# Log counts added to the attention scores in place of a mask product and a count factor, with value frames made on chip, key parts stored once, later loads of the gated stage's weights, and new orders on all engines

## The reference

```python
# 1: attention of 16 heads of width 16 over the 64 picked rows (a row may be picked more than once)
q = (layernorm(x) @ W_q.T)
c_sel = (ctx @ W_kv_down.T)[indices]
k, v = c_sel @ W_kv_up.T
attn = softmax(q . k / 4, over the 64 picks)
x = x + (attn @ v) @ W_out.T
# 2: gated linear attention of 8 heads of width 64: a dense part and one of 4 experts by a router
q1, k1, v, q2, k2 = products of layernorm(x);  k2 = softmax(k2)
gk1, gk2 = log_sigmoid(...) / 16              # decays, per token and channel
o = chunk_gla(q1, k1, v, gk1) + sum_e chunk_gla(q2 * fac_e, k2 * fac_e, v, gk2 * mask_e)
x = x + (rmsnorm(o) * norm_w * silu(g)) @ Wo
```

## Time and profile before

| what | value |
|---|---|
| median of 3 runs | 1254.29 us (1249.91 to 1254.9) |
| the profiled execution | 1254.05 us, span of its instructions 1252.6 us, so 1.45 us lie around it |
| TensorE matmul / weight load busy | 1171.6 us (94%) / 952.0 us (76%) |
| VectorE busy | 980.0 us (78%), 2026 instructions |
| ScalarE busy | 913.4 us (73%) |
| GpSimd busy | 640.3 us (51%) |
| chain that ended last | PE 85%, DMA 5%, SyncE's queue 3%, ACT 3%, DVE 2% |
| DMA | 74.82 MB, mean 60 GB/s |

### The profile page before, as it was taken

The page is one execution under the profiler, slowest core; times in us unless marked ns, Lnnn a source line. Parts: engine busy times, 40 slices in busy tenths (PEclk is TensorE's granted clock), DMA queues, the critical chain, the costliest instruction groups (busy, mean ns, idle before and its releaser), DMA issues.

```text
span 1252.6 us, 30881 instructions
## 1 busy us (share of the span) xinstructions
PE 1171.6 (94%) x12256; PEld 952.0 (76%) x12256; DVE 980.0 (78%) x2026; ACT 913.4 (73%) x2290; POOL 640.3 (51%) x632
## 2 busy tenths in 40 slices
PE   2668999999999999999999999999999999999986
PEld 1446878788887777888888788888887888878864
DVE  3655888888888888888888888888888888877642
ACT  2365778778777877777778778777787787777751
POOL 2413455655544655554456555544565555445553
PEclk7877999999999999999999999999999999999998
DMA  8233112222221222122212221222222212212111
GB/s 285 69 72 98 49 49 59 49 55 72 59 56 41 58 53 54 37 53 64 83 45 58 49 55 40 53 59 51 83 58 49 59 38 52 59 39 52 30 25 23
DMA packets 82246, 74.82 MB, mean 60 GB/s; under 512 B 33017, under 2 KB 66239, under 8 KB 82102
## 3 DMA queue, kind: packets, MB, share of 16 engines
q1 hardware_dynamic: 81670, 71.89, 22.6%
q10 hardware_dynamic: 432, 0.95, 0.2%
HBM read 39.98 MB, written 15.52 MB: 44 GB/s over the span
## 4 chain that ended last, share of the span: by engine, by line
PE 85%; DMA 5%; SPq 3%; ACT 3%; DVE 2%; POOL 1%; issue 1%; ACTq 0%; POOLq 0%; DVEq 0%
PE F L391 15%; PE F L737 5%; PE TA L684 5%; PE F L385 5%; PE F L789 5%; PE F L764 5%; PE F L725 5%; PE F L800 4%; PE F L655 3%; PE SA L673 3%; PE SA L678 3%; PE F L794 3%; PE MA L691 3%; PE F L960 3%; PE TA L385 2%; PE F L781 2%
## 5 line engine op out<-in xcount | busy, mean ns | idle before, releaser
L1334 POOL TENSOR_TENSOR ZREST<-HID,ZPARTS 128x128 f32<-128x128 f32 x32 | 13.8, 431 | 218.9 <-ACT ZPARTS L1205 218.9
L1365 POOL TENSOR_TENSOR LS<-LS,ZABS 128x1024 f32<-128x1024 f32 x32 | 75.5, 2359 | 58.0 <-ACT ZABS L1278 58.0
L673 PE MATMUL SA<-MASK,minus 128*128 128x308 bf16 x256 | 73.0, 298 | 22.0 <-DMA QS<-q_dram 20.7
L665 DVE TENSOR_REDUCE PACKED<-HOT 128x19 int32<-128x1216 bf16 x64 | 92.2, 1441 | 0.1
L1321 POOL CAST IW<-IDX 128x64 f32<-128x64 int32 x32 | 8.0, 250 | 160.9 <-DMA IDX<-idx_dram 160.9
L684 PE MATMUL TA<-CONST,EXPS 128*128 128x128 f32 x512 | 87.6, 294 | 0.8 <-ACT OT L1270 0.8
L1355 POOL TENSOR_TENSOR QM<-QD,ISEXPT 128x1024 f32<-128x1024 f32 x32 | 75.9, 2372 | 5.0 <-DMA QD<-QG 4.9
L684 PEld LDWEIGHTS TA<-CONST,EXPS 128*128 128x128 f32 x512 | 72.0, 209 | 6.5 <-issue 5.1
L1357 POOL TENSOR_TENSOR AT<-AT 128x1024 f32<-128x1024 f32 x32 | 75.9, 2371 | 0.8 <-DVE AT L1055 0.8
L1358 POOL TENSOR_TENSOR QM<-QD,ISEXPT 128x1024 f32<-128x1024 f32 x32 | 76.0, 2375 | 0.0
L678 PE MATMUL SA<-KNOW,QS 128*128 128x154 bf16 x512 | 73.1, 232 | 0.0
(11 more groups left out here) (269 smaller groups left out, 3958.7 us busy)
## 6 DMA issues: line engine op xcount, KB each, us to landing
QD<-QG SPq DMA_DIRECT2D x128, 128.0 KB, 2.4
QS<-q_dram SPq DMA_DIRECT2D x64, 192.0 KB, 3.2
q_dram<-QPARTS SPq DMA_DIRECT2D x32, 192.0 KB, 2.1
XA<-x_dram SPq DMA_DIRECT2D x32, 128.0 KB, 2.2
QS<-q_dram SPq DMA_DIRECT2D x32, 128.0 KB, 2.4
XB<-x_dram SPq DMA_DIRECT2D x32, 128.0 KB, 3.0
out_dram<-OUT SPq DMA_DIRECT2D x32, 128.0 KB, 1.7
...
```

The lines of the kernel that those rows point to most:

```text
L665: return dve.tensor_reduce(PACKED[:, r], HOT[:, r, :], AX.X, ALU.add)
L673: pe.matmul(SA[:, i, 0:2 * NKV], minus[:, :], MASK[t % 2][:, :].unsqueeze(1).to_broadcast([P, 2, NKV]), start=True, stop=False, skip_group ...
```

## The change

- The counts enter the scores. ScalarE takes `LN` = Ln(COUNT + 1e-30); GpSimd makes `OFF` (-1e30 where the count is 0) and `LNC` = LN + OFF. VectorE no longer reduces a group's scores with one instruction: for each of the four heads a `tensor_tensor_reduce` adds LNC to the 154 scores in PSUM, writes them back negated in place, and keeps their minimum. In the instruction list this is a pair: one over 154 columns and one that writes the 128x1 result. The exponentials take the scores with scale -1. The mask products, `minus`, `count_transposes`, `COUNTR`, `COUNTT` and `MASK` go, and with them the factor on the transposed exponentials: `PT` is one plain copy of 640 columns across two banks, on VectorE for groups 0 and 2 and on ScalarE for groups 1 and 3.
- The value frames are made on GpSimd; `v_frame` and its four loads go.
- Each key part is stored once (three stores for batch 0, one for the other batches together), and the slabs are read with four loads per batch (`K_RUNS`).
- The loads of the weights of stages c and d move from iteration 0 to iteration 1, behind the first keys and queries.
- The order of work within an iteration is new on all five queues.

The core of the diff:

```diff
-K_SLABS = (0, 0, 0, 1, 1, 1, 2, 2)
+K_SLABS = (0, 1, 0, 1, 2, 1, 2, 0)
+K_RUNS = ((0, 2), (2, 5), (5, 7), (7, 8))
...
-        k_dram = nc.dram_tensor("k_dram", (B * P, HA * NKV), bf16).ap()
+        k_dram = nc.dram_tensor("k_dram", (B * PARTS * DA, HA * NKV), bf16).ap()
...
+        ROWS = TM[:, :, :].rearrange("p a c -> p (a c)")[:, 0:(GH + 1) * P]
+        OUTS = MA[:, 3 * P:4 * P]
...
+        def value_ones(v):
+            ones = v[:, 0:HA * VW].rearrange("p (h w) -> p h w", w=VW)[:, :, DA]
+            rest = v[:, HA * VW:VALW].rearrange("p (g h w) -> p g h w", h=GH, w=VW)[:, :, :, DA]
+            pool.memset(ones, 1.0)
+            return pool.tensor_copy(rest, const("quarter").unsqueeze(1).to_broadcast([P, GROUPS, GH]))
...
+            pool.memset(VALL[:, :, :], 0.0).then_inc(s_zeros, 1)
+
+        def pool_frames():
+            pool.wait_ge(s_zeros, 2)
+            for n in range(RB):
+                last = value_ones(VALL[:, n, :])
+            last.then_inc(s_frame, 1)
...
-            load(sp, s_frame, (VNOW[0][:, :], v_frame))
...
-            load(sp, s_frames, *[(VALL[:, n, :], v_frame) for n in range(RB)])
...
-        def sp_k_store(b):
+        def sp_k_store_first():
             for n in range(PARTS):
-                first, end = n * PARTS, min(n * PARTS + PARTS, len(K_SLABS))
-                sp.wait_ge(s_kparts, n + 1 if b == 0 else 2 * PARTS)
-                sp.dma_start(k_rows[b, :, first:end, :],
-                             KPARTS[:, b, n, :].unsqueeze(1).to_broadcast([P, end - first, KD * NKV])).then_inc(s_krows, 16)
+                sp.wait_ge(s_kparts, n + 1)
+                sp.dma_start(k_rows[:, n, :], KPARTS[:, 0, n, :]).then_inc(s_krows, 16)
+
+        def sp_k_store_rest():
+            sp.wait_ge(s_kparts, 2 * PARTS)
+            sp.dma_start(k_rows[:, PARTS:PARTS * B, :], KPARTS[:, 1:B, :, :].rearrange("p b n w -> p (b n) w")).then_inc(s_krows, 16)
+
+        def key_slabs(n):
+            for first, end in K_RUNS:
+                m = (n * PARTS + K_SLABS[first]) * DA
+                sp.dma_start(KNOW[n % 2][first * DA:end * DA, :, :].rearrange("p h j -> p (h j)"),
+                             k_dram[m:m + (end - first) * DA, :]).then_inc(s_batch[n % 2], 16)
 
         def sp_batch_first():
             sp.wait_ge(s_krows, 16 * PARTS)
-            sp.dma_start(KNOW[0][:, :, :].rearrange("p h j -> p (h j)"), k_dram[rows(0), :]).then_inc(s_batch[0], 16)
+            key_slabs(0)
 
         def sp_batch(n):
-            sp.wait_ge(s_krows, 16 * PARTS * B)
+            sp.wait_ge(s_krows, 16 * (PARTS + 1))
             sp.wait_ge(s_vrows, 16)
...
-        def count_transposes():
-            pe.matmul(spare[:, cols(0)], COUNT[:, 0:P], identb[:, :], start=True, stop=True)
-            return pe.matmul(spare[:, cols(1)], COUNTR[:, :, :].rearrange("p j h -> p (j h)"), identb[:, :], start=True, stop=True)
...
-                pe.matmul(SA[:, i, 0:2 * NKV], minus[:, :], MASK[t % 2][:, :].unsqueeze(1).to_broadcast([P, 2, NKV]),
-                          start=True, stop=False, skip_group_check=True)
...
-                                     start=False, stop=True, skip_group_check=True)
-            return last
...
+        def maxima(t, out):
+            for h in range(GH):
+                s = score_banks[:, h // 2, h % 2, :]
+                last = dve.tensor_tensor_reduce(s, s, LNC[t % 2][:, :], -1.0, LARGE, ALU.add, ALU.min, out[:, h:h + 1])
+            return last
...
+            return pe.transpose(MA[:, 0:P], exps[:, P:NPAD, :].rearrange("p j h -> p (j h)"), ident)
...
+                maxima(b, MAXS[:, 0, :]).then_inc(s_b_max, 1)
...
+            if 0 <= d < TILES:
+                dve.wait_ge(s_d_exp1, 4 * d + 4)
+                dve.wait_ge(s_d_k1_ps, d + 1)
+                dve.tensor_tensor(flat(KG1T[:, :, :]), D2, EN1[:, :], ALU.mult).then_inc(s_d_k1, 1)
...
+                maxima(b, MAXS[:, 1, :]).then_inc(s_b_max, 1)
...
+                dve.tensor_copy(PT[0][:, :], ROWS).then_inc(s_b_probs, 1)
...
-                dve.tensor_tensor(PR[0][:, :], MA[:, 3 * P:4 * P], COUNTT[b % 2][:, 1, :], ALU.mult).then_inc(s_b_probr, 1)
-                dve.tensor_tensor(PT[0][:, :, :], TA[:, :].rearrange("p (h q) -> p h q", h=GH), COUNTT[b % 2][:, 0, :].unsqueeze(1).to_broadcast([P, GH, P]), ALU.mult).then_inc(s_b_probs, 1)
...
+            if 0 <= a < TILES:
+                dve.wait_ge(s_a_hot, 2 * a + 1)
+                dve.tensor_tensor(HOT[:, :, :], HOT[:, :, :], WEIGHT[:, :].unsqueeze(1).to_broadcast([P, BASES, PICKS]), ALU.mult).then_inc(s_a_hot, 1)
...
+                dve.wait_ge(s_b_scores, 4 * b + 3)
+                maxima(b, MAXS[:, 0, :]).then_inc(s_b_max, 1)
+            if 0 <= c < TILES:
+                dve.tensor_reduce(RT[:, 1:2], LOGIT[:, :], AX.X, ALU.max, negate=True).then_inc(s_c_router, 1)
+            if 0 <= d < TILES:
                 dve.wait_ge(s_d_a1_ps, d + 1)
                 dve.tensor_tensor(by_head(AT1), banks_12, tri.unsqueeze(1).to_broadcast([P, 2 * NP, P]), ALU.mult).then_inc(s_d_at1, 1)
...
+                dve.wait_ge(s_d_a2_ps, d + 1)
+                dve.tensor_tensor(by_head(AT2), banks_12, TRIE[d % 2][:, :].unsqueeze(1).to_broadcast([P, 2 * NP, P]), ALU.mult).then_inc(s_d_at2, 1)
...
+                act.activation(PT[1][:, :], ROWS, ACT.Copy).then_inc(s_b_probs_act, 1)
...
+                act.wait_ge(s_a_qrest, 2 * a + 1)
+                act.activation(QPARTS[:, 1, :, :], QREST[:, :, :], ACT.Copy).then_inc(s_a_qparts, 1)
+            if 0 <= b < TILES:
+                act.wait_ge(s_b_values, 4 * b + 2)
+                act.activation(OT[:, 1, :], OUTS, ACT.Copy).then_inc(s_b_ot, 1)
...
-                act.activation(MASK[a % 2][:, :], COUNT[:, 0:NKV], ACT.Relu, bias=const("masked"), scale=MASKED).then_inc(s_a_counts_act, 1)
...
+                act.activation(LN[:, :], COUNT[:, 0:NKV], ACT.Ln, bias=const("tiny")).then_inc(s_a_lncount, 1)
...
+                pool.wait_ge(s_d_dec, d + 1)
+                pool.tensor_tensor(states, states, DEC[:, 0:NS].unsqueeze(2).to_broadcast([P, NS, DK]), ALU.mult)
+                pool.wait_ge(s_d_qd, 64 * d + 64)
+                pool.tensor_tensor(QM[:, 0, :, :, :].rearrange("p a b t -> p (a b) t"), QD[:, :, :, :].rearrange("p a b t -> p (a b) t"), ISEXPT[d % 2][:, 0, :].unsqueeze(1).to_broadcast([P, H, P]), ALU.mult)
...
                 pool.wait_ge(s_a_qparts, 2 * a + 1)
                 pool.tensor_tensor(QREST[:, :, :], QT[:, :, :], QPARTS[:, 0, :, :], ALU.subtract).then_inc(s_a_qrest, 1)
             if 0 <= d < TILES:
-                pool.wait_ge(s_d_dec, d + 1)
-                pool.tensor_tensor(states, states, DEC[:, 0:NS].unsqueeze(2).to_broadcast([P, NS, DK]), ALU.mult)
-                pool.wait_ge(s_d_qd, 64 * d + 64)
-                pool.tensor_tensor(QM[:, 0, :, :, :].rearrange("p a b t -> p (a b) t"), QD[:, :, :, :].rearrange("p a b t -> p (a b) t"), ISEXPT[d % 2][:, 0, :].unsqueeze(1).to_broadcast([P, H, P]), ALU.mult)
...
+                pool.tensor_scalar(OFF[:, :], COUNT[:, 0:NKV], 0.5, MASKED, ALU.is_lt, ALU.mult).then_inc(s_a_off, 1)
...
+                pool.tensor_tensor(LNC[a % 2][:, :], LN[:, :], OFF[:, :], ALU.add).then_inc(s_a_counts_pool, 1)
...
+                    sp_k_store_first()
+                    sp_batch_first()
+                if a == 1:
                     sp_weights2()
                     sp_weights3()
...
-                    for n in range(1, B):
-                        sp_k_store(n)
+                    sp_k_store_rest()
                     sp_v_store()
```

463 lines of the change are left out of this document (210 added, 253 removed).

## The result

| | before | after |
|---|---|---|
| median | 1253.32 us (4 runs) | 1240.93 us (4 runs, 1239.66 to 1243.95) |
| ratio, with its 95% interval | | 0.9912 (0.9892 to 0.9931) |
| span of the profiled execution | 1252.6 us | 1242.6 us |

What follows compares the result with a forecast made beforehand. In the steady part TensorE was taken to bound the kernel, at 35.93 us an iteration. From 1254.05 us, 23 for the iterations and 10 for the start were taken off, giving 1221 us, range 1202 to 1252.

Steps and rivals of the forecast that it cites:

- the place of `XN`: VectorE's list ahead of XN: XN 0.27 us later, so TensorE starts its transposes 6.45 us into the iteration, before 6.18.
- These cost nothing as long as their results are early: GpSimd's two added 154-column operations, with 17 us idle, and ScalarE's added work, with 7.8 us idle, were priced at nothing.
- the 35.17 of the sum: Forecast length of a steady iteration in us, 0.76 less than the present 35.93; 23 us over 30 iterations.
- The price of the pair: VectorE's two instructions per head in the maxima: 0.30 us a pair, so a group costs 1.19 us, 0.48 more.
- The estimate from the page's overheads: Trainium skill's overheads applied to VectorE's pair: 0.125 + 0.160 + 0.060 = 0.345 us, whole kernel 1237 us.
- The lower end of 0.30: VectorE's pair costs at least 0.30 us: 0.227 for 154 columns, from PR and QG, plus 0.07 from RT.
- The dear pair: Rival on VectorE's maxima: pair at 0.33 to 0.37 (about 1237 us) chance 0.17, to 0.41 0.10, above 0.12.
- `XN` first, `AT` second: Two places where TensorE waits for VectorE: XN's transposes at 6.45 us, then the first AT, ending at 15.51 us.
- the forecast wait of 0.36 us: TensorE ahead of the second `inner`: there at 15.17 us, waits for VectorE's first AT, goes on at 15.54.
- VectorE does not bind: Rival: VectorE's chain runs ahead of TensorE's, iteration 34.54 us, whole 1202 us; chance 0.08.
- The start: First iterations: key parts land earlier, first scores 6.8 us sooner, iteration 3's QS wait covered; 10 us (4 to 14).
- `QREST` late: Rival: GpSimd's QREST, now behind QM, delays OT by 0.4 us in each of 30 iterations; 1233 us, chance 0.10.

Runs made afterwards that it cites:

- both ways of doing so: Changed kernel with SG run earlier (ScalarE's exponential of LS ahead of two VM copies), 1217.23 us; or with SG held back until VectorE made XM, 1218.50 us.
- The run with the single reduction: Changed kernel with each group's four pairs replaced by the one reduction of the kernel before, counts left out of the scores: 1230.04 us, 0.9810.
- the useless reductions: Fastest version (early SG, QREST ahead of the decays, early XA and IDX loads) plus a 128x512 constant reduction ahead of each group's maxima: 1253.45 us, 1.0001.
- both runs above: Changed kernel with the nine weight loads back in iteration 0, 1247.18 us; kernel before with weight and value-frame loads moved to iteration 1, 1245.80 us.
- the best version: Changed kernel with SG earlier, QREST ahead of the decays, and the next tile's XA and IDX loads behind the query slabs: 1207.16 us, 0.9657.

## Why the prediction was wrong

Direction and range held; the size did not: 33 us forecast, 12.4 measured, 23 forecast for the iterations and 3.4 lost there. In its own steps:

- **The step that failed** is the place of `XN`, 6.45 us after the start: it takes every operation of VectorE ahead of `XN` at its old duration, and puts GpSimd at nothing, as in "These cost nothing as long as their results are early". The sum asks when a result of GpSimd is needed, not what it runs beside, and `SG` does not occur in it. The runs showed `XN` at 7.23: `SG`, which is needed some 26 us later, had moved onto VectorE's `K`, ahead of the first maxima and `Q`, and cost 1.0 us of the 1.39 I had taken off TensorE. Moving it away gave 23.7 us by the medians (22 by the ratios, each against its own runs of before), and both ways of doing so gave the same iteration.
- **Luck.** The 1217 us that this makes is within 4 us of the forecast, but by two errors that cancel: the quiet iteration is 0.26 us shorter than the 35.17 of the sum, some 8 us in 30, and the long iterations, which the sum does not have, cost 8.5 us.
- The kernel before showed it. `QREST` took 1.58 us beside the `HOT` product, and takes 0.67 in the new order; I wrote that half of it "may be contention" and used it for `QREST` alone. Had I laid GpSimd's row beside VectorE's for each operation that the new order moves, `SG` on `K` would have been found.
- The Trainium skill states it (SBUF — State Buffer, Who interferes with whom): a VectorE operation with two SBUF inputs and a GpSimd operation that reads SBUF contend for a shared port pair, and whichever issues second is blocked to the end of the first. The traces agree in both orders: `K` 1.78 us behind `SG`, `SG` 1.71 behind `K`; and the pair with a PSUM operand is not held up.
- **The price of the pair**: 0.30 forecast, 0.275 measured. The estimate from the page's overheads (0.345) was too high, for an operation that reads and writes PSUM too. The lower end of 0.30 was wrong too, and with it the reason that less would need more than one column a cycle: at 1.04 ns a column 0.160 us are columns, and what comes on top, for both instructions, is 0.115 us, not the 0.137 of the two neighbours in my rows. The dear pair did not come.
- **`XN` first, `AT` second**: without the collision `XN` came 6.25 us after the start (forecast 6.45, of which the cheaper pairs give 0.13) and bound, as forecast. The first `AT` ended at 14.84 (forecast 15.51; 252.78 less 237.94), ahead of TensorE, which came at 15.20: the forecast wait of 0.36 us is not there, and in its place stand 0.36 us of slack. TensorE took 8.95 us from `XN` to there (8.72 in the sum) and 19.71 from there to the end (19.63). So the rival "VectorE does not bind" holds for `AT` and not for `XN`. Without the 0.28 us at `XN` the iteration would be an estimated 34.63, against 34.54 in that rival; a wait for `OT` that the sum had struck out is part of the rest (0.25 us from the last routing transpose to `OT`). No run took VectorE off that place in the quiet version.
- **The formula** 35.17 + 12 (c - 0.30) gives 34.87 for the measured 0.275, close to 34.91, but not for its reason: of its three groups only the first stood in the chain. The run with the single reduction shows it (0.36 us for one group). The other two count only once the groups have used up the 0.36 us of slack ahead of `AT`, as with the useless reductions.
- **The start**: 10 us forecast, 11.2 measured by the fourth iteration, the parts otherwise. The first scores moved by 9.6 us instead of 6.8: the key parts landed by 16.1 (17 in the sum), four loads of keys took 1.73 us to issue (2.6), and `QS` landed 3.56 us after its issue, before 5.06. Against that stands a term that the sum does not have: making the value frames keeps GpSimd from 15.04 to 18.09, ahead of the last query part, and the query store goes out at 18.73, 0.86 us after the loads of keys. The wait of 5.33 us for `QS` went, but iteration 2 to 3 is only 0.4 us shorter (38.21 against 38.63): TensorE waits there for `XN` (4.56 us) and for ScalarE instead. The place of the loads explains nearly all (both runs above). In the kernel before with that move alone the nine stores are still there and the wait for `QS` is 7.84 us, and yet the fourth iteration begins only 0.7 us later than with the whole change; why the one store is worth so little was not tried.
- **`QREST` late**: right in some iterations, 5.5 us between the fourth and the last of the profiled executions (1011.28 to 1005.80). What makes `QD` and `IDX` land a microsecond or two late in some of the iterations is open; no run took it apart. The iterations of the best version show nothing of it.
